# A graph network on one core: the scores' node numbers brought by a broadcast transfer, TensorE's score loop holding two rounds, and a fused layer split in two

## The chip, the cores and the metric

The kernel runs on one core of a Trainium2 chip. The metric is the device time of one execution in microseconds. Before the change it is 5467.57 us, the median of 3 runs (5465.55 to 5475.74). The traces are those of one profiled execution each.

A core has five engines with instruction streams of their own: TensorE (PE in the rows, with its weight loads as PEld), VectorE (DVE), ScalarE (ACT), GpSimd (POOL) and SyncE (SP). They meet only through semaphores. SBUF is the on-chip memory of 128 partitions, PSUM the small memory that TensorE writes its products to.

## The reference

3125 nodes with 128 features, 100000 edges sorted by destination, four layers, and a layer norm of the sum after each:

```
x = norm(x + L0(x))   # mean of the neighbours' rows, then relu(agg @ W1.T + b1) @ W2.T + b2
x = norm(x + L1(x))   # attention: e = edge_attr @ We; k, v = k[src] + e, v[src] + e
                      # alpha = sum over each head of q[dst] * k / sqrt(C), softmax over dst
                      # out = sum over dst of alpha * v + x @ Wskip + bskip
                      # out + gelu(gelu(out @ W1 + b1) @ W2 + b2)
x = norm(x + L2(x))   # (x + 3 * sum over edges of edge_weight * x[dst], by src) / 4
x = norm(x + L3(x))   # per edge type: messages forward (by dst) and back (by src), summed
```

All is float32.

## The kernel before

The edges are cut into 782 tiles of 128; those that share a block of 128 destination nodes form pairs of a tile and a block (806 of them). 25 blocks hold the nodes. The program is a row of stages with a barrier between them; each is a block with one function per engine:

- **Input, sort, index** and **link_nodes** (L732): edges become dense link matrices (`linked`), written to HBM.
- **linked_sum "l0"** (L845): 25 steps, each loads 1.6 MB of `linked` in two halves (SP and ACT queues), TensorE does 25 matmuls per step (L886). **mlp_layer "m0"** (L1090): 5 chunks of 5 blocks go through transpose, two matmuls, relu, layer norm.
- **project** (L1356): q and the rows of k and v, written to HBM.
- **scores** (L1426): 202 steps of four pairs (`STEP`), through a ring of six buffers (`WAYS`). For each pair GpSimd gathers 128 rows of k and v by an indirect DMA (L1481, 806 of them). SP brings the edge features (L1489) and one row of 512 block-local node numbers (`sc_locr`, L1492, 2 KB). TensorE spreads this row over 128 partitions by a product with ones (`spread_row`, L1571), turns the features (L1580), picks q by a matrix of zeros and ones (L1584) and multiplies the features by We (L1588). VectorE makes that matrix from the spread row in PSUM (`heat`, L1526), adds e to k and v (L1533), multiplies by q and sums by head (L1537, L1540). ACT copies the turned features (L1500) and stores v + e (L1505, 256 KB a step). The order within a step is written out: each engine's loop is one round of six steps, 33 rounds (`WHOLE`) and a rest of four.
- **softmax_maxima** (L1605), **weigh_values** (L1785): softmax and the weighted sum over edges, result in `skip`.
- **mlp_and_linked_sum** (L1203): after a clear of the semaphores, one stage for the attention layer's two matmuls with Gelu, its norm, and the second linked_sum (`f_links`, L1307). It works in 7 chunks (one of 1 block, six of 4), and TensorE's order interleaves the links' matmuls of a chunk with the turn, widen and narrow steps (L1291, L1296, L1301) of the chunk two on.
- **residual_norm "n2"** (L1880), **messages** (L1934), **gather_sum "g3"** and **"g4"** (L928): 782 gathers each (L983), with one matmul per block-pair (L1036) that adds them up. g3 makes the rows of the back messages beside it (`rows_of`, L1049; `bias`, L1002), unrolled over all groups. **n3** writes the output.

GpSimd has a second task: 782 record scatters (L720) prepare the order by source. `RECORD_PARTS` says how many of them stand in each stage; all must be done before the messages stage. The order of the work around the change is set by the written order of each engine's stream and by the semaphores of the rings.

Of the kernel before, what the change touches and what calls it, by code (L numbers as in the profile page):

```python
# [73 lines left out]
assert 2 * GROUP * (RING - 4) >= BLOCKS - 1 + GROUP and PAIRS_PAD % 24 == 0 and PAIRS_PAD + 2 * GROUP <= PAIR_COLS and BLOCKS % CHUNK == 0 and TILES % (2 * SCAT) == 0  # L74
# [314 lines left out]
RECORD_PARTS = {"index": 6, "link": 302, "l0": 76, "m0": 36, "project": 23, "maxima": 104, "weigh": 112, "m1": 42, "l2": 0}  # L389
# [455 lines left out]
def linked_sum(nc, S, dram, tag, which, weights=None, biases=None):  # L845
# [3 lines left out]
    with ExitStack() as stack:  # L849
# [30 lines left out]
        def _(pe):  # L880
            pe.wait_ge(cleared, 1)
            for b in range(BLOCKS):
                pe.wait_ge(landed[b % WAYS], 32 * (b // WAYS + 1))
                for k in range(BLOCKS):
                    part = links[:, b % WAYS, k * P:(k + 1) * P]
                    last = pe.matmul(ps[:, k * D:(k + 1) * D], part, S["x"][:, b * D:(b + 1) * D],  # L886
                                     start=False, stop=True, skip_group_check=True)
                last.then_inc(summed, 1)
            if which == 0:
# [38 lines left out]
def gather_sum(nc, S, dram, tag, name, table, index, fresh=True, back=False):  # L928
# [6 lines left out]
    with ExitStack() as stack:  # L935
# [9 lines left out]
        if back:  # L945
            y = m.sb(tag + "_y", [P, 2, HW])
            product, biased = m.sem(tag + "_product"), m.sem(tag + "_biased")
            saved = [m.sem(f"{tag}_saved{k}") for k in range(2)]
# [5 lines left out]
        beside = {(15 * b) // 4: b for b in range(BLOCKS)} if back else {}  # L954
# [4 lines left out]
        def keep_rows(eng, k):  # L959
            for b in range(k, BLOCKS, 2):  # L960
                eng.wait_ge(biased, (b + 1) * PIECES)
                eng.dma_start(dram["y_back"][b * P:(b + 1) * P, :], y[:, k, :]).then_inc(saved[k], 16)
            eng.wait_ge(saved[k], 16 * ((BLOCKS + 1 - k) // 2))

        @block.sync
        def _(sp):
            if back:
                keep_rows(sp, 0)

        @block.scalar  # L970
        def _(act):
            if back:
                keep_rows(act, 1)
# [13 lines left out]
        def _(dve):  # L987
# [9 lines left out]
            def bias(b):  # L997
                if b >= 2:
                    dve.wait_ge(saved[b % 2], 16 * (b // 2))
                for k in range(PIECES):  # L1000
                    dve.wait_ge(product, b * PIECES + k + 1)
                    dve.tensor_tensor(y[:, b % 2, k * PIECE:(k + 1) * PIECE], area,  # L1002
                                      S["ms_b"][:, HW + k * PIECE:HW + (k + 1) * PIECE], ALU.add).then_inc(biased, 1)

            if back:
                for n in range(GROUPS):
                    i, q = divmod(n, WAYS)
                    dve.wait_ge(summed[q], i + 1)
                    compare(q, n * GROUP)
                    if n - 1 in beside:  # L1010
                        bias(beside[n - 1])
            else:
                with dve.Fori(0, WHOLE) as i:
                    for k in range(RING):
                        dve.wait_ge(summed[k % WAYS], i * (RING // WAYS) + (k // WAYS + 1))
                        compare(k % WAYS, start_of(i, k))
                for k in range(REST):
                    dve.wait_ge(summed[k % WAYS], (WHOLE * RING + k) // WAYS + 1)
                    compare(k % WAYS, start_of(WHOLE, k))

        @block.tensor
        def _(pe):
# [20 lines left out]
            def rows_of(b, n):  # L1043

                pe.wait_ge(heated[n % WAYS], n // WAYS + 1)
                for k in range(PIECES):
                    if b or k:
                        pe.wait_ge(biased, b * PIECES + k)
# [3 lines left out]
            if back:  # L1052
                for n in range(GROUPS):
                    i, k = divmod(n, RING)
                    landed_group(i, k, lands_in(n), size(n))
                    if n in beside:
                        rows_of(beside[n], n + 1)
# [1177 lines left out]
```

## Time and profile before

| | before |
|---|---|
| median of 3 runs | 5467.57 us |
| profiled execution, its own time | 5464.14 us |
| its span in the trace | 5462.4 us |
| mean granted TensorE clock, of full speed | 0.692 |
| busy over the span: PE, DVE, ACT, POOL | 3078.4, 2227.4, 613.3, 3425.1 us |

No engine is busy over the whole span. The stages are limited by different things, so the table says little by itself; a row per stage, with the idle time of each engine and what ended it, says more. Windows in the trace are given in us from the span's start. The scores run from about 1083 to 2385, the fused stage from 2752 to 3077, g3 from 3186 to 4301 and g4 to 5426.

### The profile page before, as it was taken

Reading aid. Unit: us, or ns where it says so; the run is one execution under the profiler, and the core shown is the slowest. Engines: PE = TensorE matmul, PEld = TensorE weight load, DVE = VectorE, ACT = ScalarE, POOL = GpSimd, SP = SyncE. Lnnn points to the kernel's source line nnn. Section 1 sums busy time; section 2 is a strip of 40 time slices with the busy share of each in tenths; the row PEclk is TensorE's granted clock in tenths of the full one; section 3 lists DMA queues with packets and bytes.
Section 4 is the critical chain, followed back from the end, with each engine's and each line's share of the span. In section 5 each row is a group of like instructions: output and inputs, shape, how many; then the busy total and the mean of one; then the engine's idle time right before and its main releaser. Section 6 shows DMA issues by size and latency. Waiting matters only on the chain. (4 is left out here: it accounts for less than half of the span.)

```text
span 5462.4 us, 50006 instructions
## 1 busy us (share of the span) xinstructions
PE 3078.4 (56%) x13752; PEld 2245.2 (41%) x13755; DVE 2227.4 (41%) x2697; ACT 613.3 (11%) x1068; POOL 3425.1 (63%) x3213
## 2 busy tenths in 40 slices
PE   3899989467777777743925743433343333333333
PEld 1788879233333333323925622322232222323232
DVE  7999975445455454566911331111111110101112
ACT  0455540000000000003701000000000000000000
POOL 2888878466565655557872046666666666666664
PEclk7999999666666666656967865666666655556555
DMA  5566666144444444424924532222222111111111
GB/s 176 159 178 190 177 207 217 31 129 139 132 138 135 136 135 133 134 86 118 279 69 139 202 111 60 64 58 61 62 59 60 49 46 45 46 47 46 48 44 47
DMA packets 498516, 599.50 MB, mean 110 GB/s; under 512 B 190097, under 2 KB 367423, under 8 KB 496101
## 3 DMA queue, kind: packets, MB, share of 16 engines
q0 software_dynamic: 117856, 246.12, 16.7%
q1 hardware_dynamic: 337605, 229.37, 15.0%
q10 hardware_dynamic: 42944, 122.68, 6.0%
q8 instruction: 51, 0.84, 0.1%
q14 instruction: 60, 0.49, 0.0%
HBM read 406.29 MB, written 204.36 MB: 112 GB/s over the span
## 5 line engine op out<-in xcount | busy, mean ns | idle before, releaser
L1036 PE MATMUL ps<-g_got,g_hot 128*128 x3224 | 692.6, 367 | 1174.3 <-issue 775.9
L720 POOL DMA_INDIRECT rec_by_src<-rec,pos x782 | 1130.3, 1445 | 349.0 <-issue 239.3
L1036 PEld LDWEIGHTS ps<-g_got,g_hot 128*128 128x128 f32 x3224 | 607.2, 271 | 1269.5 <-issue 1268.4
L1481 POOL DMA_INDIRECT sc_kv<-kv,d_src x806 | 764.0, 948 | 527.1 <-issue 270.6
L983 POOL DMA_INDIRECT g_got<-y_forward,d_msg x782 | 739.6, 946 | 427.0 <-issue 230.8
L983 POOL DMA_INDIRECT g_got<-y_back,s_msg x782 | 739.6, 946 | 385.1 <-issue 231.6
L805 PE MATMUL ps<-ln_low,ln_hot 128*125 128x256 f32 x2848 | 619.0, 380 | 20.0 <-DVE ln_low L782 16.8
L805 PEld LDWEIGHTS ps<-ln_low,ln_hot 128*125 128x125 f32 x2848 | 534.8, 188 | 104.1 <-issue 24.1
L994 DVE TENSOR_TENSOR g_hot<-ps,src_loc 128x1024 f32<-128x1024 f32 x101 | 120.8, 1222 | 995.6 <-remote 672.1
L1588 PE MATMUL ps<-w_e,sc_attrT 128*128 128x512 f32 x404 | 324.4, 898 | 256.0 <-ACT sc_attrT L1500 211.7
L1002 DVE TENSOR_TENSOR g_y<-ps,ms_b 128x384 f32<-128x384 f32 x75 | 41.8, 558 | 863.0 <-remote 527.9
L1584 PE MATMUL ps<-q,sc_hotT 128*128 x1616 | 312.4, 356 | 74.6 <-issue 36.0
L1533 DVE TENSOR_TENSOR sc_kve<-sc_kv,ps 128x1024 f32<-128x1024 f32 x202 | 245.0, 1213 | 252.9 <-DMA win_rows<-rec_by_dst,win_tilei 173.9
L1584 PEld LDWEIGHTS ps<-q,sc_hotT 128*128 128x128 f32 x1616 | 287.6, 266 | 96.6 <-issue 96.6
L1571 PE MATMUL ps<-sc_locr,ones 1*128 1x512 f32 x404 | 320.7, 884 | 10.4 <-issue 10.4
L1526 DVE TENSOR_SCALAR sc_hotT<-ps,part 128x512 f32<-128x512 f32 x202 | 148.0, 747 | 356.0 <-PE ps L1571 201.9
L1049 PE MATMUL ps<-ms_w,ms_xT 128*128 128x384 f32 x150 | 111.3, 832 | 284.2 <-DVE g_y L1002 193.0
L1919 ACT ACTIVATE n_root<-n_var 128x25 f32<-128x25 f32 x2 | 0.5, 226 | 2333.0 <-DVE n_var L1908 2333.0
L777 DVE TENSOR_TENSOR ln_low<-col,win_lo 128x1024 f32<-128x1024 f32 x178 | 219.3, 1232 | 4.0 <-PE ps L805 1.8
L782 DVE TENSOR_TENSOR ln_low<-ln_low,win_w 128x1024 f32<-128x1024 f32 x178 | 216.3, 1215 | 0.0
L779 DVE TENSOR_TENSOR ln_hot<-col,win_key 128x1000 f32<-128x1000 f32 x178 | 214.0, 1202 | 0.0
L1869 PE MATMUL ps<-wv_ve,wv_hot 128*128 128x128 f32 x1616 | 188.5, 279 | 40.8 <-DVE wv_ve L1845 37.2
(315 smaller groups left out, 3249.5 us busy)
## 6 DMA issues: line engine op xcount, KB each, us to landing
linked<-ln_out SPq DMA_DIRECT2D x320, 224.0 KB
ve<-sc_kve ACTq DMA_DIRECT2D x202, 256.0 KB
wv_ve<-ve SPq DMA_DIRECT2D x101, 512.0 KB
l_links<-linked SPq DMA_DIRECT2D x25, 800.0 KB
l_links<-linked ACTq DMA_DIRECT2D x25, 800.0 KB
f_links<-linked SPq DMA_DIRECT2D x25, 800.0 KB
f_links<-linked ACTq DMA_DIRECT2D x25, 800.0 KB
attr_pairs<-ln_feats POOLq DMA_DIRECT2D x7, 2048.0 KB
```

The source lines that it names most:

```text
L720: pool.indirect_dma_start(out=dram["rec_by_src"], out_offset=bass.IndirectOffsetOnAxis(ap=S["pos"][:, c:c + 1], axis=0), in_=S["rec"][:, c ...
L777: dve.tensor_tensor(low[:, q, :, 0:P], S["col"][:, :].unsqueeze(1).to_broadcast([P, GROUP, P]), S["win_lo"][:, cols].unsqueeze(2).to_broad ...
L779: dve.tensor_tensor(hot[:, q], S["col"][:, 0:KEYS].unsqueeze(1).to_broadcast([P, GROUP, KEYS]), S["win_key"][:, cols].unsqueeze(2).to_broa ...
L782: dve.tensor_tensor(low[:, q, :, P:2 * P], low[:, q, :, 0:P], S["win_w"][:, cols].unsqueeze(2).to_broadcast([P, GROUP, P]), ALU.mult).then ...
L805: last = pe.matmul(ps[0:KEYS, bass.ds(slots[j], 2 * P)], hot[:, q, j, :], low[:, q, j, :], start=False, stop=True, skip_group_check=True)
L983: pool.indirect_dma_start(out=got[:, (c % SLOTS) * D:(c % SLOTS + 1) * D], out_offset=None, in_=table, in_offset=bass.IndirectOffsetOnAxis ...
L1036: last = pe.matmul(ps[:, bass.ds(columns[j], width)], hot[:, q, j, :], got[:, bass.ds(slots[j], width)], start=False, stop=True, skip_grou ...
L1481: pool.indirect_dma_start(out=kv[:, q, j, :], out_offset=None, in_=dram["kv"], in_offset=bass.IndirectOffsetOnAxis(ap=S["d_src"][:, c:c + ...
L1533: dve.tensor_tensor(kve[:, q].rearrange("p a (k d) -> p k a d", d=D), kv[:, q].rearrange("p k (a d) -> p k a d", a=2), feat(q).rearrange(" ...
L1571: pe.matmul(spread_loc(q), S["ones"][0:1, :], locr[0:1, q, :], start=True, stop=True).then_inc(spread[q], 1)
L1584: pe.matmul(qe(q)[:, j * D:(j + 1) * D], hot_t[:, q, j * P:(j + 1) * P], S["q"][:, bass.ds(cols[j], D)], start=True, stop=True)
L1588: pe.matmul(feat(q), attr_t[:, q % 2, :], S["w_e"][:, :], start=True, stop=True).then_inc(product[q], 1)
```

## The change

1. **scores.** SP no longer brings the row of 512 numbers to one partition but to all 128, by a broadcast read from HBM into `sc_locb` [128, 6, 512]: 256 KB a step, 202 of them. The matmul that spread the row (L1571) is gone, with its semaphores; `heat` compares `sc_locb` in SBUF, and SP waits for `heated` in place of `spread` before it refills a buffer. TensorE's and VectorE's loops hold two rounds of six steps instead of one.
2. **The fused stage is split.** `mlp_layer("m1")` (5 chunks of 5 blocks, the function of m0 with Gelu) runs after weigh_values and before the clear; `linked_sum("l2")` after it. `skip` moves to the layer's memory.
3. **linked_sum**: TensorE's 25 steps become a loop of four with a rest of one.
4. **g3**: TensorE's and VectorE's streams become the loop that g4 has, with the back messages at two groups in eight; ACT copies the block that they read (`xs`), and SP alone stores the result.
5. **RECORD_PARTS**: m0 36 to 24, project 23 to 20, m1 42 to 20, l2 81 to 118.

The core of the diff:

```
-RECORD_PARTS = {"index": 6, "link": 302, "l0": 76, "m0": 36, "project": 23, "maxima": 104, "weigh": 112, "m1": 42, "l2": 0}
+RECORD_PARTS = {"index": 6, "link": 302, "l0": 76, "m0": 24, "project": 20, "maxima": 104, "weigh": 112, "m1": 20, "l2": 0}
...
@@ linked_sum, TensorE @@
-            for b in range(BLOCKS):
-                pe.wait_ge(landed[b % WAYS], 32 * (b // WAYS + 1))
...
+            with pe.Fori(0, BLOCKS // WAYS) as i:
+                for q in range(WAYS):
+                    add(i, q)
+            for q in range(BLOCKS % WAYS):
+                add(BLOCKS // WAYS, q)
...
@@ gather_sum @@
-        beside = {(15 * b) // 4: b for b in range(BLOCKS)} if back else {}
+        beside = {1: 0, 5: 1} if back else {}
...
+                    act.activation(xs[:, b % 2, :], S["x_t"][:, b * D:(b + 1) * D], ACT.Copy).then_inc(copied[b % 2], 1)
...
+            with pe.Fori(0, WHOLE) as i:
+                for k in range(RING):
+                    landed_group(i, k, GROUP)
+                    if k in beside:
+                        rows_of(i, beside[k], k + 1)
...
-def mlp_and_linked_sum(nc, S, dram, weights, biases):
...
@@ scores, SP @@
-                sp.wait_ge(spread[q], i + 1)
-                sp.dma_start(locr[0:1, q, :], dram["loc"][n * STEP:(n + 1) * STEP, :].rearrange("(a k) e -> a (k e)", a=1)).then_inc(placed[q], 16)
+                sp.wait_ge(heated[q], i + 1)
+                sp.dma_start(locb[:, q, :], dram["loc"][n * STEP:(n + 1) * STEP, :].rearrange("(a k) e -> a (k e)", a=1)
+                             .to_broadcast([P, STEP * P])).then_inc(placed[q], 16)
...
@@ scores, VectorE @@
-                dve.wait_ge(spread[q], i + 2)
+                dve.wait_ge(placed[q], (i + 1) * 16)
                 dve.wait_ge(product[q], i + 1)
-                dve.tensor_scalar(hot_t[:, q, :], spread_loc(q), S["part"][:, 0:1], None, ALU.is_equal).then_inc(heated[q], 1)
+                dve.tensor_scalar(hot_t[:, q, :], locb[:, q, :], S["part"][:, 0:1], None, ALU.is_equal).then_inc(heated[q], 1)
...
-            with dve.Fori(1, WHOLE) as i:
+            for i in range(1, 1 + (WHOLE - 1) % 2):
                 round_of(i, i)
+            with dve.Fori(0, (WHOLE - 1) // 2) as twice:
+                for k in range(2):
+                    i = twice * 2 + (1 + (WHOLE - 1) % 2 + k)
+                    round_of(i, i)
...
@@ scores, TensorE @@
-            def spread_row(i, q):
-                pe.wait_ge(placed[q], (i + 1) * 16)
-                before_last(pe, heated, q, i)
-                pe.matmul(spread_loc(q), S["ones"][0:1, :], locr[0:1, q, :], start=True, stop=True).then_inc(spread[q], 1)
...
-            with pe.Fori(0, WHOLE) as i:
+            for i in range(WHOLE % 2):
                 for q in range(WAYS):
                     step(i, q)
-                    if q + 2 < WAYS:
-                        spread_row(i, q + 2)
-                    else:
-                        spread_row(i + 1, q + 2 - WAYS)
+            with pe.Fori(0, WHOLE // 2) as twice:
+                for k in range(2):
+                    i = twice * 2 + (WHOLE % 2 + k)
+                    for q in range(WAYS):
+                        step(i, q)
...
@@ gnn_kernel @@
-        S["skip"] = m.sb("skip", [P, BLOCKS * D])
...
+            S["skip"] = a.sb("skip", [P, BLOCKS * D])
...
+            mlp_layer(nc, S, dram, "m1", False)
...
-                mlp_and_linked_sum(nc, S, dram, ins["L3_gnn_weights"], ins["L3_gnn_biases"])
+                linked_sum(nc, S, dram, "l2", 1, ins["L3_gnn_weights"], ins["L3_gnn_biases"])
```

TensorE's rows in one step of the scores, before (L1571 is the spread, L1580 the turn, L1584 the four picks of q, each with a register instruction ahead, L1588 the product with We):

```order
L1584 ISA
L1584 MATMUL ps<-q,sc_hotT 128x128
L1588 MATMUL ps<-w_e,sc_attrT 128x512
L1571 MATMUL ps<-sc_locr,ones 128x512
L1575 ISA
L1575 TENSOR_LOAD dst_steps
L1580 MATMUL ps<-ident,sc_attr 128x128
```

and after (the same lines are L1427, L1431 and L1435; `dst_steps` holds the block numbers):

```order
L1431 ISA
L1431 MATMUL ps<-q,sc_hotT 128x128
L1435 MATMUL ps<-w_e,sc_attrT 128x512
L1422 TENSOR_LOAD dst_steps
L1427 MATMUL ps<-ident,sc_attr 128x128
L1431 ISA
```

The spread's row between two steps is gone, and with it one wait for a transfer and one for VectorE. The rest keeps its order.

TensorE in the fused stage before, from its second chunk on (L1307 are the links' matmuls):

```order
L1291 MATMUL ps<-ident,skip 128x128 x4
L1296 MATMUL ps<-f_aggT,w_l 128x512
L1301 MATMUL ps<-w_l,f_hidT 128x128 x4
L1307 MATMUL ps<-x_rows,f_links 128x128 x25
L1291 MATMUL ps<-ident,skip 128x128 x4
L1296 MATMUL ps<-f_aggT,w_l 128x512
L1301 MATMUL ps<-w_l,f_hidT 128x128 x4
L1307 MATMUL ps<-x_rows,f_links 128x128 x25
L1291 MATMUL ps<-ident,skip 128x128 x4
L1307 MATMUL ps<-x_rows,f_links 128x128 x25
L1296 MATMUL ps<-f_aggT,w_l 128x512
L1307 MATMUL ps<-x_rows,f_links 128x128 x25
```

and where m1 ends and l2 follows, after:

```order
L1185 MATMUL ps<-w_l,m_hidT 128x128 x5
L1177 MATMUL ps<-m_aggT,w_l 128x320 x2
L1185 MATMUL ps<-w_l,m_hidT 128x128 x5
L1099 UNCONDITIONAL_BRANCH
L879 UNCONDITIONAL_BRANCH
L890 UNCONDITIONAL_BRANCH
L890 ISA
L886 ISA
L886 MATMUL ps<-x_rows,l_links 128x128 x25
L886 ISA
```

The links' matmuls no longer stand between the layer's steps; all of them come behind the last chunk, in a loop.

GpSimd between softmax_maxima and the messages, before (L720 are record scatters, L88 the clear):

```order
L1663 UNCONDITIONAL_BRANCH
L720 DMA rec_by_src<-rec,pos 100096x4 x104
L1611 UNCONDITIONAL_BRANCH
L1829 UNCONDITIONAL_BRANCH
L720 DMA rec_by_src<-rec,pos 100096x4 x112
L1791 UNCONDITIONAL_BRANCH
L88 ISA
L1249 UNCONDITIONAL_BRANCH
L720 DMA rec_by_src<-rec,pos 100096x4 x123
L1209 UNCONDITIONAL_BRANCH
```

and after:

```order
L1506 UNCONDITIONAL_BRANCH
L720 DMA rec_by_src<-rec,pos 100096x4 x104
L1454 UNCONDITIONAL_BRANCH
L1672 UNCONDITIONAL_BRANCH
L720 DMA rec_by_src<-rec,pos 100096x4 x112
L1634 UNCONDITIONAL_BRANCH
L1160 UNCONDITIONAL_BRANCH
L720 DMA rec_by_src<-rec,pos 100096x4 x20
L1099 UNCONDITIONAL_BRANCH
L88 ISA
L919 UNCONDITIONAL_BRANCH
L720 DMA rec_by_src<-rec,pos 100096x4 x118
L849 UNCONDITIONAL_BRANCH
```

20 scatters move ahead of the clear, 118 stay behind it, where 123 were.

## Rows read from the trace of the kernel before

**Rows 1.** The scores' lines by form: busy, mean ns | idle before, releasers.

```profile
L1481 POOL DMA_INDIRECT sc_kv<-kv,d_src x806 | 764.0, 948 | 527.1 <-issue 270.6 <-DVE sc_kve L1533 232.6 <-DVEq L1521 23.8
L1571 PE MATMUL ps<-sc_locr,ones 1*128 1x512 f32 x404 | 320.7, 884 | 10.4 <-issue 10.4
L1526 DVE TENSOR_SCALAR sc_hotT<-ps,part 128x512 f32<-128x512 f32 x202 | 148.0, 747 | 356.0 <-PE ps L1571 201.9 <-issue 64.7 <-remote 63.5
```

**Rows 2.** Windows by stage: length, busy by engine, clock, DMA share, GB/s.

```profile
785.00:957.00 172.00, 150.22 (x1300) 151.38 (x1300) 97.07 (x29) 0.00 (x0) 138.87 (x76) 0.91 0.75 240
957.00:1033.00 76.00, 26.39 (x95) 20.50 (x95) 31.03 (x111) 9.48 (x16) 35.55 (x36) 0.57 0.02 1
1083.00:2385.00 1302.00, 961.78 (x2627) 459.05 (x2628) 656.69 (x810) 56.09 (x202) 764.01 (x806) 0.65 0.46 132
2752.00:3077.00 325.00, 172.32 (x1339) 162.43 (x1339) 33.67 (x113) 31.72 (x42) 120.20 (x123) 0.73 0.41 135
4303.00:5440.00 1137.00, 395.33 (x1672) 346.08 (x1672) 124.57 (x105) 0.00 (x0) 739.60 (x782) 0.58 0.18 45
```

**Rows 3.** Timeline, one score step at half clock: start, length, instruction.

```profile
1532.34 2.07 PE L1571 MATMUL ps<-sc_locr,ones 1*128 1x512 f32 x2
1534.61 1.91 PE L1584 MATMUL ps<-q,sc_hotT 128*128 x8
1538.16 1.22 PE L1571 MATMUL ps<-sc_locr,ones 1*128 1x512 f32 x1
```

**Rows 4.** Timeline, one score step at full clock.

```profile
1506.29 1.12 PE L1571 MATMUL ps<-sc_locr,ones 1*128 1x512 f32 x2
1509.35 1.12 PE L1571 MATMUL ps<-sc_locr,ones 1*128 1x512 f32 x2
```

**Rows 5.** Timeline, one round of six steps with its void.

```profile
1514.35 1.15 PE L1584 MATMUL ps<-q,sc_hotT 128*128 x8
1522.90 2.08 PE L1588 MATMUL ps<-w_e,sc_attrT 128*128 128x512 f32 x2 [7.40 <-ACT sc_attrT L1500]
1551.85 1.15 PE L1584 MATMUL ps<-q,sc_hotT 128*128 x8
```

**Rows 6.** Waits of the scores (1100 to 2340): total, times, longest.

```profile
POOL sc_kv L1481 <- DVE sc_kve L1533: 232.6, 79, 8.1
```

**Rows 7.** DMA queue of ACT's stores in the scores: packets, MB, share.

```profile
q10 hardware_dynamic: 27659, 50.37, 10.7%
```

**Rows 8.** Timeline, record scatters beside VectorE.

```profile
793.07 3.49 DVE L905 TENSOR_TENSOR l_degree<-l_degree,l_links 128x3200 f32<-128x3200 f32 x1
793.57 3.84 POOL L720 DMA_INDIRECT rec_by_src<-rec,pos  x1 [0.30 <-issue]
2394.39 0.58 DVE L1710 TENSOR_SCALAR mx_bad<-mx_loc 128x816 f32<-128x816 f32 x1 [9.51 <-DMA mx_loc<-loc]
2394.43 1.38 POOL L720 DMA_INDIRECT rec_by_src<-rec,pos  x1 [0.30 <-issue]
```

**Rows 9.** Timeline, starts and ends of l0 and of the fused stage.

```profile
785.25 15.06 SPq L865 DMA_DIRECT2D l_links<-linked  x5
933.69 1.42 PEld L892 LDWEIGHTS ps<-ones,l_degree 128*128 128x128 f32 x12
2763.38 0.97 POOL L720 DMA_INDIRECT rec_by_src<-rec,pos  x1 [11.43 <-POOLq L89]
3076.92 3.49 DVE L1898 SCALAR_TENSOR_TENSOR n_t<-ps,x_rows 128x3200 f32<-128x3200 f32 x1 [44.71 <-PEq L1209]
```

**Rows 10.** Table loads in the fused stage, by line.

```profile
L1262 ACT ACT_TABLE_LOAD x7 | 9.0, 1283 | 0.1
```

**Rows 11.** Timeline and window, TensorE's slow matmuls, fused stage and g4.

```profile
2908.65 0.37 PE L1307 MATMUL ps<-x_rows,f_links 128*128 128x128 f32 x1 [2.43 <-issue]
4426.00:4448.00 22.00, 3.55 (x9) 0.50 0.19 48
```

More of the change, by code:

```diff
@@ L881, in _, with add @@
             pe.wait_ge(cleared, 1)
-            for b in range(BLOCKS):
-                pe.wait_ge(landed[b % WAYS], 32 * (b // WAYS + 1))
+            def add(i, q):
+                pe.wait_ge(landed[q], i * 32 + 32)
                 for k in range(BLOCKS):
-                    part = links[:, b % WAYS, k * P:(k + 1) * P]
-                    last = pe.matmul(ps[:, k * D:(k + 1) * D], part, S["x"][:, b * D:(b + 1) * D],
-                                     start=False, stop=True, skip_group_check=True)
+                    last = pe.matmul(ps[:, k * D:(k + 1) * D], links[:, q, k * P:(k + 1) * P],
+                                     S["x"][:, bass.ds(i * (WAYS * D) + q * D, D)], start=False, stop=True, skip_group_check=True)
                 last.then_inc(summed, 1)
+            with pe.Fori(0, BLOCKS // WAYS) as i:
[3 more added lines that the diff above has]
+                add(BLOCKS // WAYS, q)
             if which == 0:
@@ L946, in gather_sum @@
             y = m.sb(tag + "_y", [P, 2, HW])
+            xs = m.sb(tag + "_xs", [P, 2, D])
             product, biased = m.sem(tag + "_product"), m.sem(tag + "_biased")
+            copied = [m.sem(f"{tag}_copied{k}") for k in range(2)]
             saved = [m.sem(f"{tag}_saved{k}") for k in range(2)]
@@ L967, in _ @@
             if back:
-                keep_rows(sp, 0)
+                for b in range(BLOCKS):
+                    sp.wait_ge(biased, (b + 1) * PIECES + 1)
+                    sp.dma_start(dram["y_back"][b * P:(b + 1) * P, :], y[:, b % 2, :]).then_inc(saved[b % 2], 16)
+                for h in range(2):
+                    sp.wait_ge(saved[h], 16 * ((BLOCKS + 1 - h) // 2 + 1))
         @block.scalar
@@ L972, in _ @@
             if back:
-                keep_rows(act, 1)
+                for b in range(BLOCKS):
+                    if b >= 2:
+                        act.wait_ge(product, (b - 1) * PIECES)
+                    act.activation(xs[:, b % 2, :], S["x_t"][:, b * D:(b + 1) * D], ACT.Copy).then_inc(copied[b % 2], 1)
         @block.gpsimd
@@ L1445, in scores @@
             "kept", "heated", "product", "added", "multiplied", "scored", "saved"))
-        spread = [m.sem(f"sc_spread{h}") for h in range(WAYS)]
         cleared = m.sem("sc_cleared")
@@ L1565, in _ @@
                 pe.sem_inc(product[q], 1)
-                pe.sem_inc(spread[q], 1)
-            def spread_row(i, q):
-                pe.wait_ge(placed[q], (i + 1) * 16)
-                before_last(pe, heated, q, i)
-                pe.matmul(spread_loc(q), S["ones"][0:1, :], locr[0:1, q, :], start=True, stop=True).then_inc(spread[q], 1)
             def step(i, q):
```

212 lines of the change are left out of this document (31 added, 181 removed).

## The prediction

> **What bounds the kernel now.** I read the windows by stage first [rows 2], then the scores' instructions by line and form [rows 1], their waits [rows 6], single steps and rounds on the timeline [rows 3 to 5], and last the places that resemble what the change makes. A measurement of this kernel can tell a change from none at about 0.2%, 11 us.
>
> The scores take 1302 us of 5462, and no engine is busy throughout: TensorE 962, VectorE 657, GpSimd 764 [rows 2]. GpSimd's gathers last 0.948 us and stand idle for 527.1 us before them [rows 1]. Part of that is spacing: two of its DMAs in a row have 0.30 us between them [rows 8]. 806 x (0.948 + 0.30) = 1006 us is thus the floor of this stage for GpSimd, and 527.1 - 806 x 0.30 = 285 us is real waiting; 232.6 of it is for the buffers that VectorE frees (L1533) [rows 6], 23.8 for the start of the stage [rows 1]. VectorE in its turn waits 201.9 us ahead of its comparison for TensorE's spread [rows 1]. So the chain of a step is spread, comparison, picks on TensorE, sum on VectorE, buffer free, gather, and TensorE is the one who is late.
>
> How late, the timeline tells. At half clock (1.2 GHz) one step runs from spread to spread in 1538.16 - 1532.34 = 5.82 us, and the spread's two matmuls are 2.07 of it [rows 3]; I count 2.0. At full clock (2.4 GHz) a step is 1509.35 - 1506.29 = 3.06 us with 1.12 of spread [rows 4]. GpSimd needs 4 x 1.248 = 4.99 us per step: between the two. Once in a round there is a void, here 7.40 us in which TensorE waits for ACT's copy [rows 5]. From pick to pick over a round it is 1551.85 - 1514.35 = 37.5 us for six steps [rows 5], 6.25 us a step; GpSimd would need 30. 202 x 6.25 = 1263 us is the stage without its edges.
>
> **The change, part by part.**
>
> *Scores, TensorE.* It removes 404 matmul records of 0.884 us, 320.7 us of TensorE [rows 1]. A step at half clock becomes 5.82 - 2.0 = 3.8 us, at full clock about 2.0. Even a round all at half clock and with a void of 8 us is 6 x 3.8 + 8 = 31 us, and with the void in every second round 6 x 3.8 + 4 = 27, under GpSimd's 30. So TensorE is no longer the late one and GpSimd's floor is next. Of the 285 us of waiting, the start's 24 stay; 261 can go at most.
>
> *What keeps the 261 from going whole.* First, the comparison reads SBUF now and not PSUM. The trace has such an operation: VectorE's comparison of 816 columns from SBUF took 0.58 us, and the scatter that GpSimd had just begun took 1.38 in place of 0.97 [rows 8, 9]. By columns the new comparison is 0.58 x 512 / 816 = 0.36 us (an estimate), against 0.747 before [rows 1]. Its price to GpSimd is between nothing (it falls into the spacing, or after the part that needs the port) and 0.41 us a step, 202 x 0.41 = 83 us. I take 0.2 us, half, as the operation is shorter than that of the row: +40 us. The Trainium skill ("SBUF — State Buffer", "Who interferes with whom") states that a tensor_scalar between SBUF operands can enter a mode with both ports, and that it and GpSimd's descriptor writing then block each other for the whole instruction; this speaks against the change, and by it the price would be at most 202 times the comparison's length. The trace agrees in kind: 3.84 us for a scatter beside a sum of 3.49 us [rows 8].
>
> Second, TensorE can be late in spite of its arithmetic. In g4, where GpSimd is the bound in the same way, the stage's 1137 us hold 739.6 of gathers and 782 x 0.30 = 235 of spacing [rows 2]: 163 us are waits, at a mean clock of 0.58. They come from stretches in which TensorE gets through one matmul in over a microsecond: 9 records in 22 us at half clock [rows 11]. In the new scores a ring of six steps, 30 us, stands between, TensorE is busier than in g4, and after such a stretch it gains 1.2 us a step at half clock and 3 at full clock. The price lies between 0 and 163 x 806 / 782 = 168 us; I take a quarter, 40 us, as before the change the scores show one void of 7.4 us a round and no such stretch in the round that I read.
>
> *Scores, the rest.* The broadcast writes 256 KB a step where 2 KB went. ACT's store of v + e has the same 256 KB and took 10.7% of the DMA engines over the stage [rows 7]; the share would go from 0.46 to about 0.57 [rows 2]. It is asked for as soon as the buffer's last comparison is done, up to six steps (30 us) ahead: hidden. If that cover fails, VectorE waits for `placed`. The larger loops add nothing to a step; they halve the number of loop ends. VectorE loses 0.39 us a step and was not late.
>
> Sum for the scores: -261 + 40 + 40 = -181 us, from 1302 to 1121.
>
> *The fused stage.* Before, from 2752 to the first operation of n2 at 3076.92 are 325 us [rows 2, 9], of which 11 are the clear [rows 9]; TensorE is busy only 172 of it [rows 2]. After, three pieces. m1: the same function as m0, which took 76 us [rows 2]. It loses the averaging (three operations per chunk) and gains two Gelus, a sum and the reading of tables, 1.283 us each [rows 10], at most 10 x 1.283 = 13 us, mostly asked for while ACT waits. I take 80 us; bounds 60 (m0's window holds waits that need not come again) and 115 (tables on the path, and a slow stretch of TensorE of 22 us [rows 11]). The clear: 11 us. l2: in l0 the time from the first link transfer to the last link matmul is 933.69 - 785.25 = 148 us at 0.91 of the clock [rows 2, 9], with 25 times 1.6 MB of transfers; the same in l2, with 5 for the weights behind them: 153. GpSimd's 118 scatters at 0.97 + 0.30 = 1.27 us make 150 beside it. Together 80 + 11 + 153 = 244: -81 us. That l2 gets what l0 has rests on the loads not waiting for matmuls: in the fused stage those wait for the layer's norm of each chunk, and slow matmuls stand there, too (a gap of 2.43 us before one [rows 11]). From 60 + 11 + 148 = 219 to 115 + 11 + 215 = 341 (the 215 in the rivals) the piece is worth -106 to +16.
>
> *g3.* GpSimd's gathers bound it; the products and the biases keep their number. With the loop, the back messages come at two groups in eight. I take 0, within 25 us on either side, since the waits of the like stage g4 are 163 us and the loop there is the same. *l0's loop, RECORD_PARTS:* m0's 36 scatters take 35.55 of 76 us [rows 2]; 12 fewer change nothing there. The three that leave project were beside other work: 0.
>
> **Sum.** -181 - 81 = -262 us, on the profiled execution: 5464 - 262 = 5202. The median of the runs is 3.4 us above that execution: 5205.
>
> **The rivals.**
>
> *B, the bare floor.* The comparison costs GpSimd nothing and TensorE is never late: -261 - 81 = -342, 5126 us. For it: the step has 0.30 us of spacing four times, and rings of six. Against: 0.41 us in the row [rows 8].
>
> *A, the waits of g4 come to the scores.* 168 us of waits in place of my 40: 5205 + 128 = 5333 us. For it: the spread kept TensorE busy (962 of 1302 us), and without it it is at 641 of 1121, 57%, nearer to g4's 395 of 1137 [rows 2]. Against: the ring, and that it catches up fast. The Trainium skill ("TensorE: Matmul & The Clock Gate", "HAM oscillation") says that an engine which waits for data between bursts falls back to the low clock each time; by this the scores would stay at half clock, which alone costs nothing, as 3.8 us is under 4.99.
>
> *D, l2's scatters are slowed as l0's were.* In l0 76 scatters took 138.87 us, 1.83 each [rows 2], beside a sum of two SBUF operands that l2 has not. If the slowing came from the link transfers, 118 x 1.83 = 215 us in place of 153: 5205 + 62 = 5267. Against: the lone 3.84 beside the sum [rows 8].
>
> *C, slower.* Slow matmuls take over the scores. A step has 11 records; the slow window of g4 shows 9 in 22 us [rows 11], and records can be missing from a trace: at 16 in 22 us, the two for each of a group's eight pairs, a step is 15 us. With a share f of the stage's time so spent, the rest at 3.8, the step is 1 / (f/15 + (1-f)/3.8). With the 81 us from the split against it, the kernel is slower once a step exceeds 6.25 + 81/202 = 6.65 us, which is f = 0.57. At f = 0.6 the step is 6.9 us, the stage +135, the kernel +54: 5522 us. For it: such stretches exist in g4. Against: in g4 the waits are 163 us only, and none filled the scores before.
>
> **How the numbers follow.** My forecast 0.62 (5150 to 5290, rival D within it at 0.05), B 0.15, A 0.15, C 0.05, and 0.03 for something I don't see. The likeliest gives 5205. The range leaves out C, and the outer halves of A and B: 5130 to 5325. Faster by over 0.2%: all but C and part of the unseen, 0.93; within 0.2%: 0.02; slower: 0.05.
>
> **What would show it.** In the profile after, the scores' window should be near 1120 us, GpSimd's gathers with about 0.95 to 1.0 us each and waits for VectorE under 80 us; TensorE should now wait for the comparison or the features, not the reverse. A gather mean near 1.05 would speak for the port's full price; gathers at 0.948 for none. m1 should read about 80 us, l2 about 153 with 1.27 us per scatter; 1.8 per scatter is D. If the scores' window is over 1200 us with TensorE's records a microsecond and more apart, A or C holds. If g3 differs by over 25 us, my zero there was wrong. The forecast as a whole is wrong if the scores keep over 1250 us.

## The result and the profile after

The change did not make the kernel faster. On the first chip it takes 5474.12 us, the median of 20 runs (5464.37 to 5482.80), beside 5466.97 us before (5455.19 to 5475.74, 20 runs): ratio 1.0014, 95% interval 1.0008 to 1.0021. Run again on a second chip, with the experiments below, it takes 5420.06 us beside 5453.03: 0.9936 (0.9914 to 0.9959). An interval holds for the repeats on one chip; between chips the ratio moves by more. From -0.6% to +0.1% is what is known of the change, where -262 us, -4.8%, were forecast.

The stages by the two profiled executions, read from the timeline (a gather stage from its first gather's start to its last one's end):

| | before, us | after, us | forecast |
|---|---|---|---|
| first gather of the scores starts | 1087.5 | 1072.3 | no change |
| scores, gathers | 1267.2 | 1251.8 | -181 |
| last matmul of weigh_values to first operation of n2 | 330.2 | 365.4 | -81 |
| of it: linked_sum l2, matmuls | | 285.7 | 148 |
| g3, gathers | 1115.6 | 1117.2 | 0 |
| g4, gathers | 1112.2 | 1112.9 | 0 |

The 148 us of the forecast counted from the first link transfer; the matmuls alone, l0's as the model, are 142. The first line is a small gain ahead of the scores, where m0 has 24 scatters beside it in place of 36; the scores gain 15 us; the split loses 35 us. Between g3's last gather and g4's first, 12.5 us became 20.5, which I have not explained.

The windows by stage of the changed kernel, columns as in [rows 2] (m0; scores; m1; clear and l2; g4):

```profile
962.00:1023.00 61.00, 25.06 (x97) 19.69 (x98) 31.46 (x112) 9.47 (x16) 24.36 (x24) 0.64 0.02 1
1068.00:2349.00 1281.00, 575.79 (x2222) 356.59 (x2222) 603.56 (x809) 55.97 (x202) 767.50 (x806) 0.70 0.61 176
2711.00:2783.00 72.00, 27.68 (x95) 21.10 (x95) 32.23 (x101) 24.82 (x30) 23.27 (x23) 0.62 0.01 1
2783.00:3076.00 293.00, 160.96 (x1250) 154.75 (x1250) 3.47 (x1) 0.00 (x0) 114.23 (x118) 0.73 0.44 149
4317.00:5450.00 1133.00, 383.94 (x1652) 337.95 (x1650) 124.18 (x105) 0.00 (x0) 737.76 (x782) 0.58 0.17 46
```

In the scores TensorE is busy 576 us in place of 962 [rows 2], and the gathers take 1252 us in place of 1267. The lines of the scores, as in [rows 1]:

```profile
L1330 POOL DMA_INDIRECT sc_kv<-kv,d_src x806 | 767.5, 952 | 508.1 <-DVE sc_kve L1383 248.1 <-issue 236.2 <-DVEq L1371 23.8
L1431 PE MATMUL ps<-q,sc_hotT 128*128 x1616 | 287.0, 333 | 363.1 <-issue 309.7 <-DVE alpha_cols L1390 26.8 <-DVE sc_hotT L1376 25.6
L1435 PE MATMUL ps<-w_e,sc_attrT 128*128 128x512 f32 x404 | 292.1, 814 | 332.2 <-ACT sc_attrT L1350 258.7 <-issue 73.5
L1376 DVE TENSOR_SCALAR sc_hotT<-sc_locb,part 128x512 f32<-128x512 f32 x202 | 94.5, 496 | 5.8 <-DMA sc_locb<-loc 5.8
```

The two lines of TensorE's other matmuls in the kernel before:

```profile
L1584 PE MATMUL ps<-q,sc_hotT 128*128 x1616 | 312.4, 356 | 74.6 <-issue 36.0 <-DVE sc_hotT L1526 32.6 <-DVE alpha_cols L1540 5.5
L1588 PE MATMUL ps<-w_e,sc_attrT 128*128 128x512 f32 x404 | 324.4, 898 | 256.0 <-ACT sc_attrT L1500 211.7 <-issue 44.3
```

The gathers wait 248.1 us for VectorE's buffers where they waited 232.6 before [rows 6]. The work taken from TensorE came back as idle time ahead of its other matmuls: 363.1 and 332.2 us, where 74.6 and 256.0 stood before. A void of the changed kernel on the timeline shows how:

```profile
1307.44 0.95 POOL L1330 DMA_INDIRECT sc_kv<-kv,d_src  x1 [0.30 <-issue]
1309.75 2.07 PE L1435 MATMUL ps<-w_e,sc_attrT 128*128 128x512 f32 x2 [2.81 <-issue]
1311.62 0.42 PE L1427 MATMUL ps<-ident,sc_attr 128*128 128x128 f32 x1
...
1317.44 0.95 POOL L1330 DMA_INDIRECT sc_kv<-kv,d_src  x1 [0.30 <-issue]
1321.55 0.28 ACT L1350 ACTIVATE sc_attrT<-ps 128x128 f32<-128x128 f32 x1 [11.85 <-remote]
1321.57 1.22 DVE L1383 TENSOR_TENSOR sc_kve<-sc_kv,ps 128x1024 f32<-128x1024 f32 x1 [11.43 <-DMA dst_rows<-rec_by_dst,pair_tiles]
...
1323.54 0.94 POOL L1330 DMA_INDIRECT sc_kv<-kv,d_src  x1 [5.15 <-DVE sc_kve L1383]
...
1324.79 1.16 POOL L1330 DMA_INDIRECT sc_kv<-kv,d_src  x1 [0.30 <-issue]
```

TensorE's transpose is drawn at 1311.62 and its product at 1309.75. ACT, which waits for the transpose, and VectorE, which waits for the product and for its gathers, both go on at 1321.5 only (the name that the second row gives for VectorE's releaser is not to be relied on, as it waited for several). The trace's record of the semaphores decides it: TensorE's product is counted at 1321.49 and its transpose at 1321.53. So TensorE's results came about 10 us later than its rows suggest (ends of matmuls are modelled in this trace). Meanwhile GpSimd issues gathers without a pause, runs out of buffers, and stands for 5.15 us. The 7.40 us of [rows 5] look like such a void, too: there ACT goes on at 1522.57 after 11.53 us, and GpSimd stood for 2.98 us.

In l2 the slowness appears with no other engine at work but GpSimd with its scatters. The link transfers wait for the matmuls, so the DMA share falls to 0.09:

```profile
2788.00:2800.00 12.00, 9.37 (x67) 9.37 (x68) 0.00 (x0) 0.00 (x0) 8.99 (x10) 0.78 1.01 329
2800.00:2936.00 136.00, 21.58 (x62) 16.35 (x61) 0.00 (x0) 0.00 (x0) 101.37 (x105) 0.51 0.09 22
2936.00:2948.00 12.00, 2.69 (x8) 2.19 (x8) 0.00 (x0) 0.00 (x0) 0.00 (x0) 0.50 0.39 136
2948.00:3075.00 127.00, 126.87 (x1113) 126.59 (x1113) 0.00 (x0) 0.00 (x0) 0.00 (x0) 0.98 0.74 264
```

67 matmul records in the first 12 us, 62 in the next 136, 1113 in the last 127. Within the 136 us a weight load or a matmul comes every 0.7 or 1.4 us:

```profile
2835.35 0.96 POOL L720 DMA_INDIRECT rec_by_src<-rec,pos  x1 [0.30 <-issue]
2835.74 0.29 PEld L886 LDWEIGHTS ps<-x_rows,l_links 128*128 128x128 f32 x1 [2.52 <-issue]
2836.62 0.97 POOL L720 DMA_INDIRECT rec_by_src<-rec,pos  x1 [0.30 <-issue]
2837.14 0.37 PE L886 MATMUL ps<-x_rows,l_links 128*128 x1 [2.43 <-issue]
```

Its start in windows of 2 us, with TensorE's busy time (and count), granted clock, DMA share and GB/s:

```profile
2798.00:2800.00 2.00, 1.12 (x11) 1.00 0.89 310
2800.00:2802.00 2.00, 0.78 (x4) 1.00 1.02 302
2804.00:2806.00 2.00, 0.55 (x2) 0.50 0.05 11
```

The matmuls are rare already while the full clock is granted; the clock falls after them. It is not the loading of instructions either: in the 170 us from 2790 on, the DMA queues of that kind moved 3 packets. The last scatter ended at 2935.7, the stretch about 11 us later. This gave the theory that I call G: GpSimd's DMAs, issued one behind the other without a pause, slow TensorE. Its rivals were K (the rise and fall of TensorE's clock brings the slow stretches) and I (instructions come slowly the first time a loop is run).

### The profile page after: what moved, and what is told of

Same layout as the page of the kernel before. It is cut to its first block and busy times, and to the rows that moved or that the text cites. A ratio compares the mean times of both kernels' runs of the same rounds, so it can differ in the third digit from the quotient of the medians.

```text
span 5471.7 us, 49525 instructions
## 1 busy us (share of the span) xinstructions
PE 2771.5 (51%) x13354; PEld 2184.7 (40%) x13357; DVE 2173.8 (40%) x2686; ACT 613.7 (11%) x1081; POOL 3418.0 (62%) x3213
## 5 line engine op out<-in xcount | busy, mean ns | idle before, releaser
L1044 PE MATMUL ps<-g_got,g_hot 128*128 x3224 | 752.8, 381 | 1330.6 <-issue 999.7
L720 POOL DMA_INDIRECT rec_by_src<-rec,pos x782 | 1124.1, 1438 | 384.3 <-issue 238.9
L1044 PEld LDWEIGHTS ps<-g_got,g_hot 128*128 128x128 f32 x3224 | 635.9, 278 | 1467.6 <-issue 1466.5
L1330 POOL DMA_INDIRECT sc_kv<-kv,d_src x806 | 767.5, 952 | 508.1 <-DVE sc_kve L1383 248.1
L1431 PE MATMUL ps<-q,sc_hotT 128*128 x1616 | 287.0, 333 | 363.1 <-issue 309.7
L1435 PE MATMUL ps<-w_e,sc_attrT 128*128 128x512 f32 x404 | 292.1, 814 | 332.2 <-ACT sc_attrT L1350 258.7
L1431 PEld LDWEIGHTS ps<-q,sc_hotT 128*128 128x128 f32 x1616 | 252.6, 238 | 491.6 <-issue 491.6
L886 PE MATMUL ps<-x_rows,l_links 128*128 (+1 forms) x2500 | 303.5, 282 | 156.6 <-issue 124.1
L886 PEld LDWEIGHTS ps<-x_rows,l_links 128*128 128x128 f32 x2500 | 297.1, 198 | 163.4 <-issue 163.4
L1435 PEld LDWEIGHTS ps<-w_e,sc_attrT 128*128 128x128 f32 x404 | 81.4, 251 | 345.4 <-ACT sc_attrT L1350 265.5
L1712 PEld LDWEIGHTS ps<-wv_ve,wv_hot 128*128 128x128 f32 x1616 | 185.7, 193 | 41.9 <-issue 41.8
## 6 DMA issues: line engine op xcount, KB each, us to landing
sc_locb<-loc SPq DMA_DIRECT2D x202, 256.0 KB
ve<-sc_kve ACTq DMA_DIRECT2D x202, 256.0 KB
```

The lines of the kernel that those rows point to most:

```text
L720: pool.indirect_dma_start(out=dram["rec_by_src"], out_offset=bass.IndirectOffsetOnAxis(ap=S["pos"][:, c:c + 1], axis=0), in_=S["rec"][:, c ...
L886: last = pe.matmul(ps[:, k * D:(k + 1) * D], links[:, q, k * P:(k + 1) * P], S["x"][:, bass.ds(i * (WAYS * D) + q * D, D)], start=False, s ...
L1044: last = pe.matmul(ps[:, bass.ds(columns[j], width)], hot[:, q, j, :], got[:, bass.ds(slots[j], width)], start=False, stop=True, skip_grou ...
L1330: pool.indirect_dma_start(out=kv[:, q, j, :], out_offset=None, in_=dram["kv"], in_offset=bass.IndirectOffsetOnAxis(ap=S["d_src"][:, c:c + ...
L1431: pe.matmul(qe(q)[:, j * D:(j + 1) * D], hot_t[:, q, j * P:(j + 1) * P], S["q"][:, bass.ds(cols[j], D)], start=True, stop=True)
L1435: pe.matmul(feat(q), attr_t[:, q % 2, :], S["w_e"][:, :], start=True, stop=True).then_inc(product[q], 1)
```

## Experiments

Where a kernel's whole time matters its ratio stands with its interval; stages are read from the profiled execution.

### 1. l2 without scatters

```
-... "m1": 20, "l2": 0}
+... "m1": 138, "l2": 0}
```

> The changed kernel with GpSimd's 118 record scatters of l2 moved into m1 (RECORD_PARTS m1 138, l2 0). In the changed kernel l2's matmuls took 286 us, of which some 148 us were one stretch with an instruction of TensorE every 0.7 to 1.4 us; it ended about 10 us after the last scatter. Theory G (GpSimd's back-to-back DMAs slow TensorE): l2 takes 142 to 150 us with no slow stretch; m1, which now has scatters beside it for 175 us, is no faster than before. Theory K (each rise and fall of TensorE's clock brings a slow stretch) and theory I (TensorE's instructions come slowly the first time a loop is run): l2 stays at 280 us or so, though no scatter stands in it, and the total grows by about 140 us.

Measured 0.9930 (0.9910 to 0.9950), 5420.9 us. The windows are m1 and l2:

```profile
2695.00:2876.00 181.00, 27.11 (x95) 20.39 (x95) 29.70 (x100) 24.93 (x30) 135.16 (x138) 0.53 0.03 2
2885.00:3030.00 145.00, 141.39 (x1248) 141.40 (x1249) 0.74 (x1) 0.00 (x0) 0.00 (x0) 0.97 0.81 294
```

l2's matmuls take 142 us in place of 286, though it is the same loop, run for the first time as before. K and I fall for l2. In m1 TensorE's part, which took 50 us beside 20 scatters, now takes 140 us beside 138: the slowness went with the scatters. The total did not grow: the changed kernel takes 5420 us in experiment 12, on another chip.

### 2. A pause between GpSimd's DMAs

```
+                    if c:
+                        pool.wait_ge(paused, c)
+                    pool.memset(pause[:, :], 0.0).then_inc(paused, 1)
```

after each gather of the scores, and the same ahead of each scatter of l2; `pause` is [128, 256].

> The changed kernel with a memset of 256 columns by GpSimd after each gather of the scores and ahead of each scatter of l2, which makes the distance between its DMAs longer by an estimated 0.3 to 0.5 us. Theory G: TensorE's slow stretches become few, l2 goes from 286 to about 118 x 1.65 = 195 us or to its transfers' 148, and GpSimd's waits of 250 us in the scores shrink to under 60; the scores then take about 806 x 1.6 = 1290 us, set by GpSimd's own pace. Theories K and I: l2 stays at 280 or more; in the scores the voids of TensorE (about 10 us, four in 75 us) stay, and the stage takes over 1350 us.

Measured 0.9715 (0.9683 to 0.9748), 5301.6 us. GpSimd's lines in the scores:

```profile
L1336 POOL DMA_INDIRECT sc_kv<-kv,d_src x806 | 776.0, 963 | 159.8 <-issue 135.8 <-DVEq L1380 24.0
L1340 POOL MEMSET sc_pause<- 128x256 f32 x806 | 276.5, 343 | 0.4
```

The wait for VectorE is gone from the line, all 248 us of it. The gathers are 0.963 + 0.343 + 0.17 = 1.476 us apart, 1.45 at the median, and the stage takes 1186 us, not the 1290 that I expected, as the distance is shorter than the 1.6 us I had put in. GpSimd does more and is done 66 us earlier than in the first profile of the changed kernel, 36 us earlier than in its second (experiment 12). In l2 the scatters stand 1.47 us apart and TensorE is slowed in part, 207 us.

### 3. More work for TensorE, and VectorE beside l2

```
+                for _ in range(2):
+                    pe.matmul(ps[:, 6 * BANK:7 * BANK], S["ident"][:, :], S["w_e"][:, :], start=True, stop=True)
```

at the end of each step of the scores; in l2 the sums into `degree` that l0 has.

> The changed kernel with two more matmuls of 512 columns per step of the scores, into an unused bank, that nobody waits for, and in l2 the 25 sums of two SBUF operands by VectorE that l0 has. Theory K: with the filler TensorE is busy 4 of 5 us at full clock, the clock falls less often, and the scores come down from 1252 us to 1100 or less; l2 stays at 286. Theory G: the filler makes the scores no faster (1250 or more); in l2 VectorE's sums slow GpSimd's scatters to about 1.8 us each, as in l0, and TensorE's matmuls then take about 145 us without a slow stretch. Theory I: neither changes.

Measured 0.9920 (0.9892 to 0.9949), 5418.1 us. The windows are the scores and l2:

```profile
1075.00:2343.00 1268.00, 860.77 (x2961) 472.33 (x2962) 584.59 (x787) 54.86 (x198) 767.43 (x805) 0.84 0.62 176
2800.00:2949.00 149.00, 142.65 (x1250) 142.47 (x1250) 93.12 (x27) 0.00 (x0) 129.23 (x65) 0.96 0.90 292
```

In the scores the mean granted clock rose from 0.70 to 0.84, TensorE was busy 861 us, and the gathers took 1270 us. The filler is work as well as clock, so this is not a test of the clock alone; but theory K expected 1100 or less. Experiment 1 has the same scores without the filler on the same chip: TensorE busy 576 us, gathers 1228. So 285 us more work made the stage 42 us longer. In l2 VectorE's sums stretch the scatters (65 of them in 149 us, 2.3 us each), and TensorE is at full pace, 142.7 us of matmuls. The other scatters run on until 3019, so from weigh_values' last matmul to n2 it is still 295 us, where the changed kernel has 365 and 368. This is why l0 was fast, from which I had taken l2's price: not in spite of VectorE's sum, but by it.

### 4. The fused stage put back

In the changed kernel `mlp_and_linked_sum` takes the place of m1 and l2.

> The changed kernel with the fused stage of before in place of m1 and l2; all else as after the change. By the two traces the stretch from the end of weigh_values to n2 took 330 us before and 365 after. If the split costs these 35 us, this kernel is about 30 us faster than the changed one (5440); all theories expect this, but by theory G the gain depends on where the slow stretches fall, so that 0 to 60 us are possible.

Measured 0.9927 (0.9903 to 0.9951), 5416.3 us. From weigh_values' last matmul to n2 it has 347 us; the changed kernel has 363 in experiment 11, on the same chip, and 368 in experiment 12, on another. By that the split by itself costs 16 to 21 us, less than the 30 expected but within the 0 to 60. The rest of the first profile's 35 us goes with the scatters: this kernel has 138 of them beside its fused stage, the kernel before 123, and experiment 10, which keeps the 123, has 329 us.

### 5 and 6. Other lengths of the pause

The edit is that of experiment 2, in g3 and g4 as well; only the columns differ.

> The changed kernel with a memset by GpSimd after each gather or ahead of each scatter, of another length in each stage: scores 128 columns, l2 512, g3 128, g4 256. With 256 columns the distance between gathers was 1.448 us and TensorE kept up. Theory G, that the rate of GpSimd's DMAs is what slows TensorE: where the distance is 1.32 us (scores, g3), either there are few slow stretches and the stage takes count x 1.32 (scores 1080, g3 1045), or they come back in part and the stage stays near 1150 to 1220 in the scores, 1090 in g3. g4 at 1.45 us: 782 x 1.45 = 1134 us, the same as without the pause (1122), with almost no waits. l2 with 118 x 1.72: its scatters take 203 us and its matmuls are done earlier, by 150 to 170 us. A rival, that a pause is only waiting moved to another place: every stage takes as long as without, or longer by the pause.

> As the run with pause lengths 128, 512, 128, 256, but scores 192 columns, l2 384, g3 192, g4 64. Theory G: scores at a distance of 1.38 us take 806 x 1.38 + 15 = 1127 us, g3 782 x 1.38 = 1080, l2's scatters 118 x 1.59 = 188 us with matmuls done within 170; g4 at 1.26 us is as without a pause, 1122, since the rate is the same. The rival expects no stage under its time without a pause.

Measured 0.9820 (0.9801 to 0.9839), 5365.7 us, and 0.9704 (0.9685 to 0.9723), 5304.7 us. All lengths together, with the median distance between the starts of GpSimd's DMAs (without a pause from the first profile, l2's 384 and 512 as measured in experiments 6 and 5):

| stage, from | distance, us | stage, us |
|---|---|---|
| scores, changed kernel | 1.25 | 1252, again 1222 |
| scores, pause of 128 | 1.34 | 1211 |
| scores, 192 | 1.39 | 1182 |
| scores, 256 | 1.45 | 1186 |
| g3: none, 128, 192 | 1.25, 1.34, 1.39 | 1117, 1125, 1120 |
| g4: none, 64, 256 | 1.25, 1.28, 1.44 | 1113, 1120, 1127 |
| l2's matmuls: none, 256, 384, 512 | 1.27, 1.47, 1.57, 1.68 | 286, 207, 142, 142 |

The scores with 128 columns are in the second of the two cases that the expectation left open. With 192 they missed: 1182 us, where I had expected 1127. The wait for VectorE's buffers shrinks step by step, from 248.1 us to 102.0 and 27.0, and to none with 256, but the memsets take its place. l2 came out as theory G had it, a little faster. g3 and g4 missed it: g3 was to come down to 1090 or 1045 with 128 columns and to 1080 with 192, and did not. Without a pause the same chip gives 1114 us for g3 and 1109 to 1112 for g4 (experiments 7 and 8), so the pause costs them 6 to 18 us. Whether GpSimd waits by itself or for TensorE, 782 gathers take 1.42 to 1.44 us each. g4 with 256 columns shows it:

```profile
L999 POOL DMA_INDIRECT g_got<-y_back,s_msg x782 | 743.4, 951 | 155.5 <-issue 128.7 <-ACTq L946 26.7
L1004 POOL MEMSET g_pause<- 128x256 f32 x782 | 256.3, 328 | 0.5
```

There is no wait left for another engine within the stage, and no gain. So for g3 and g4 the rival holds. In the scores 40 to 70 us are won. That this is because there TensorE's delay goes through ACT and VectorE before a buffer is free is my reading; no run separates it.

### 7. The kernel before with the pause

> The kernel before with the memset of 256 columns after each gather of the scores and ahead of the scatters of the fused stage; nothing else of the change. Theory G: the scores go from 1267 to 1170 to 1200 us here, too, although TensorE still spreads the numbers, since the waits came from the gathers' rate and not from the spread; the fused stage from 314 to 250 to 280. If the spread had bounded them as I forecast, the scores stay at 1260, as a step at half clock is 5.82 us.

Measured 0.9696 (0.9674 to 0.9717), 5294.0 us; the scores take 1188 us with the spread on TensorE and loops of one round, the changed kernel with the same pause 1186. This is the plainest sign that the step of my forecast was wrong: the gathers' waits for VectorE go from 232.6 us to 18.6 with the spread's 320 us still on TensorE. The fused stage goes from 314 to 234 us, more than expected.

### 8. One long pause per step

> The changed kernel with one memset of 768 columns after every four gathers of the scores in place of one of 256 after each: the mean rate is nearly the same (5.7 us in place of 5.79 for four), but within a step the gathers stand 1.25 us apart. If the mean rate over some us decides, the scores take 1160 to 1190 us; if the distance of neighbours does, TensorE's voids stay and the stage takes over 1220. l2 has no pause here and stays at 286 us.

Measured 0.9870 (0.9853 to 0.9888), 5394.2 us, l2 285 us, the scores 1183 us. The gathers within a step stand 1.25 us apart, and their wait for VectorE is 40 us in place of 248: of the two cases, the mean rate decides. l2, which has no pause here, stayed as slow as expected.

### 9. Fewer scatters in l2

With a pause of 192 columns in the scores and 384 in l2, and

```
-"l0": 76, "m0": 24, "project": 20, ... "weigh": 112, "m1": 20 (l2: 118)
+"l0": 80, "m0": 26, "project": 23, ... "weigh": 122, "m1": 25 (l2: 94)
```

> The changed kernel with a memset of 192 columns after each gather of the scores and of 384 ahead of each scatter of l2, and 24 scatters moved out of l2 (l0 80, m0 26, project 23, weigh 122, m1 25, l2 94). Theory G: scores 1185 us; l2's matmuls take 142 us and its scatters 94 x 1.59 = 149 us, 38 less than with 118; the kernel takes 5265 to 5280 us. If the scatters moved to weigh and l0 lengthen those stages instead, it stays at 5300.

Measured 0.9646 (0.9624 to 0.9668), 5251.2 us, the fastest kernel here. The windows are the scores and l2:

```profile
1083.00:2251.00 1168.00, 614.74 (x2222) 386.26 (x2222) 608.78 (x803) 56.08 (x202) 1006.32 (x1611) 0.71 0.68 192
2700.00:2856.00 156.00, 141.28 (x1250) 141.29 (x1250) 8.36 (x20) 1.61 (x3) 132.63 (x188) 0.94 0.90 279
```

l2's matmuls and scatters now end together, at 2856, as the forecast wanted them. The scores came out 17 us shorter than expected, the kernel 14 us under its range.

### 10 and 11. The broadcast alone, and loops of one round

> The kernel before with the broadcast in the scores alone: no spread matmul, loops of one round, nothing else changed. My forecast gave this part -181 us. Theory G: the gathers' rate sets the stage, which stays within 1220 and 1265 us (1267 before), and the kernel takes 5420 to 5465.

> The changed kernel with loops of one round of six steps in the scores, for TensorE and VectorE. If the loop's end costs something (a rival that would explain the voids), the scores take longer than the 1252 us with two rounds; by theory G they stay within 1220 to 1270.

Measured 0.9908 (0.9881 to 0.9934), 5395.4 us, scores 1225 us; and 0.9953 (0.9936 to 0.9970), 5424.2 us, scores 1224 us. Put into the kernel before, the broadcast alone brings 53 us on this chip, 25 more than the best that theory G expected, where I had forecast 181. In the stages I see 42 of them (1225 against 1267), but the 1267 is from another chip. What the rest of the change adds costs 29 us (5424.2 against 5395.4).

### 12 and 13. The changed kernel again, and the fastest with loops of one round

> The changed kernel itself, as it is. Its scores took 1252 us in its first profile; with the same code for the scores they took 1228 and 1220 us beside other edits, and 1224 us with loops of one round. If the larger loops cost something, this run shows about 1250 again and a ratio to before near 1.00; if the difference is one of executions or of chips, it shows 1220 to 1230.

> The fastest kernel so far (pauses of 192 columns in the scores and 384 in l2, 24 scatters moved) with loops of one round in the scores. If the loops' size matters only through GpSimd's rate, there is no difference: scores 1168 us, 5240 to 5260 in all. If loops of two rounds cost 27 us by themselves, it is that much faster: 5225.

Measured 0.9936 (0.9914 to 0.9959), scores 1222 us; and 0.9646 (0.9624 to 0.9667), 5253.8 us, scores 1167 us. With one round or two the scores are the same on these chips (1224 and 1222 us; 1167 and 1168), and experiments 1 and 4, with two rounds on the chip of the 1224, have 1228 and 1220: the size of the loops does nothing. The 1252 us of the first profile are the same program on another chip.

## Why the prediction was wrong

*"TensorE is the one who is late", for its work.* Late it was, but for the most part not for its work. I read the half-clock step (5.82 us, [rows 3]) as TensorE's price for its instructions and took 2.0 of it away. What I read as the bound was a loop: GpSimd's gathers at 1.25 us slow TensorE until the buffers run out, GpSimd stops, TensorE recovers. Such a loop settles at a rate that depends little on what TensorE has to do: with the spread and a pause the stage takes 1188 us, without the spread and with the same pause 1186 (experiments 7 and 2), and without a pause 285 us more work cost 42 (experiment 3). The rows to see it were there: the round that I read had a void of 7.40 us ([rows 5]) in which TensorE, ACT and VectorE all stood still, and I priced it as a constant to be absorbed by the ring, without asking what it was. I also held that the waits of g4 ([rows 2]: 163 us) would come only in part. They look like the same thing: g3, g4 and the scores before all need 1.42 to 1.57 us per gather, where the engine could do 1.25. In g4, though, the pause took the waits away and won nothing. Of the 163 us some 25 are the stage's ends: from first gather to last it is 1112.2 - 739.6 - 782 x 0.30 = 138.

*The scores, -181.* Measured -15 and, on the second chip, 1222 us. The 40 us that I left for waits came out at 508.1 - 806 x 0.30 - 23.8 = 242 us, nearly all of the 261 that I let go. With 3 us for the port that gives -261 + 242 + 3 = -16, the measured figure.

*The port's price, +40.* The comparison takes 0.496 us, not 0.36, and the mean gather went from 0.948 to 0.952 us: 806 x 0.004 = 3 us. Too high, and my lower bound of nothing was near. The Trainium skill's rule ("SBUF — State Buffer", "Who interferes with whom") that such an operation may block GpSimd's descriptors is seen in single gathers of the scores only, not in their sum: in the trace after 19 of the 806 take over 1.1 us (1.16 for the one at 1324.79), each of them beside a comparison, and in the kernel before none does. The scatter of 3.84 us [rows 8], which I put beside that rule, stands beside a sum, another operation; the one of 1.38 us beside a comparison was the row to compare with.

*The split, -81.* Measured +35. m1 was right: 72 us against 80. l2 was wrong: 286 us of matmuls against the 142 of l0. I took l0 as the model and named the condition, loads that do not wait for matmuls, but not the one that counted: in l0 VectorE holds GpSimd's scatters back (1.83 us each, [rows 2]), in l2 nothing does. That the sums are what spares l0 is shown by putting them into l2 (experiment 3). Rival D thought that scatters slowed by transfers would make the stage long; it is the other way round, and scatters at full speed do.

*Rivals.* A named the right place, TensorE getting through its matmuls one by one, and two thirds of the size (168 of 242 us); it did not name GpSimd's rate as the cause. C had the right kind of cause, TensorE slow for a large part of a stage, but in l2 and not in the scores. By C's sum the scores would have grown; they did not, and I read that as GpSimd stopping when its buffers are full. (The sum had a slip: at f = 0.6 a step is 6.88 us, which makes the stage +128 and the kernel +47.) A loss in l2 and A's waits in the scores together give no gain, and the range, cut at 5325 us, did not hold that.

*g3 and the ends.* g3's zero was right (1.6 us). The 15 us ahead of the scores I had at nothing, since I took m0 to be indifferent to its scatters. It takes 61 us beside 24 of them, 76 beside 36 [rows 2]; by theory G that is TensorE, faster beside fewer, but no run tests it alone.

*The clock.* The Trainium skill ("TensorE: Matmul & The Clock Gate", "HAM oscillation") explains slow matmuls by clock changes after idle gaps. The trace agrees that the clock falls after such gaps (around the void shown above it is 1.00 from 1304 to 1308 and 0.50 from 1312 on), but this is not what bounded the kernel: in l2 the slow stretch begins at full clock and the fall follows it, and experiment 3 raised the clock of the scores from 0.70 to 0.84 (with more work, too) and the stage got no shorter.

Left open: which resource GpSimd's DMAs and TensorE share. GpSimd's own activity is not it, since in experiment 9 it is busy 1006 of 1168 us, with memsets between its gathers, and TensorE keeps up. It slows TensorE and not ACT's copy or VectorE's sum of the scores, which last 0.28 and 1.20 to 1.22 us from one end of the stage to the other. Smaller or fewer descriptors per DMA were not tried. Open, too, is why g3 and g4 gain nothing from the pause, and why 1.57 us between scatters leaves l2 at full pace where 1.47 does not. Nor is the difference between the chips explained.

## What to carry to other kernels

Where GpSimd issues indirect DMAs back to back, look for weight loads and matmuls that come singly, 0.7 or 1.4 us apart, and for voids after which several engines go on at the same moment. If they are there, GpSimd's rate is the lever to try before TensorE's own work, which moved the stage by about a seventh of its size here (42 us for 285). A memset of some 200 to 400 columns between the DMAs gave 3%, and 3.5% together with some of them moved to other stages. Try it stage by stage: the two gather stages with no such ring of engines lost 6 to 18 us by it. When a stage is taken as the model for another, list what runs beside it on every engine, also what seems to hurt it.

## What the runs showed of the hardware

- TensorE beside GpSimd's indirect DMAs: at 1.27 us between them 62 matmul records took 136 us in l2 and all its matmuls 286 us; at 1.47 us they take 207, at 1.57 and 1.68 us 142, as with no scatters. The slowing began some 16 us after the first scatter in l2 and ended 11 us after the last. The Trainium skill ("SBUF — State Buffer", "Who interferes with whom") says that at SBUF's ports PE and ACT never wait on anyone. By that alone TensorE would not be slowed; the runs show that it is, and not whether it is at those ports or elsewhere.
- The mean rate over a step counts, not the distance of neighbours: four gathers 1.25 us apart and then one memset of 768 columns did as well as a pause after each.
- The same two programs had ratios of 1.0014 and 0.9936 on two chips, each with an interval of 0.0023 or less to either side.
